# Second attention of a gated cross-attention block: VectorE's batch steps move one tick later, behind the next tile's bound, maxima and sums

## What is computed

```python
def _L1_xattn_ref(Q, K, V, mask, Wq_w, Wq_b, Wk_w, Wk_b, Wv_w, Wv_b, Wo_w, Wo_b):
    q = (Q @ Wq_w + Wq_b).reshape(b, tq, H, DK).transpose(0, 2, 1, 3)
    k = (K @ Wk_w + Wk_b).reshape(b, tk, H, DK).transpose(0, 2, 1, 3)
    v = (V @ Wv_w + Wv_b).reshape(b, tk, H, DK).transpose(0, 2, 1, 3)
    scores = jnp.einsum('bhqd,bhkd->bhqk', q, k) / jnp.sqrt(jnp.float32(DK))
    scores = jnp.where(mask == 0, jnp.float32(-1000000000.0), scores)
    attn = jax.nn.softmax(scores, axis=-1)
    out = jnp.einsum('bhqk,bhkd->bhqd', attn, v)
    return out.transpose(0, 2, 1, 3).reshape(b, tq, c) @ Wo_w + Wo_b
...
x = x + jnp.tanh(g_ffn[0]) * _L0_ffn_ref(_layernorm(x), ...)
x = x + jnp.tanh(g_xattn[1]) * _L1_xattn_ref(_layernorm(x), ctx, ctx, mask, ...)
x = x + jnp.tanh(g_ffn[1]) * _L1_ffn_ref(_layernorm(x), ...)
```

## Time and profile before

| | |
|---|---|
| median of 3 runs | 790.95 us (789.13 to 792.21) |
| the profiled execution's own time | 795.5 us |
| its span | 793.9 us |
| mean granted TensorE clock in it | 0.918 |
| PE busy | 643.7 us (81%) |
| DVE busy | 454.7 us (57%) |
| ACT busy | 307.5 us (39%) |
| POOL busy | 228.4 us (29%) |

### The profile page before, as it was taken

The page is one execution under the profiler, slowest core; times in us unless marked ns, Lnnn a source line. Parts: engine busy times, 40 slices in busy tenths (PEclk is TensorE's granted clock), DMA queues, the critical chain, the costliest instruction groups (busy, mean ns, idle before and its releaser), DMA issues. The chain is left out here.

```text
span 793.9 us, 14350 instructions
## 1 busy us (share of the span) xinstructions
PE 643.7 (81%) x4685; PEld 585.7 (74%) x4686; DVE 454.7 (57%) x1167; ACT 307.5 (39%) x533; POOL 228.4 (29%) x351
## 2 busy tenths in 40 slices
PE   3798943999999996788554757778997799999997
PEld 3566632989998996777443535558996689999997
DVE  5845555774447543000378888666657575565566
ACT  7544312552336333323453442444333323343331
POOL 7531443010001001000374854645003601011053
PEclk9999965999999999989777888788998999999999
DMA  7999316751006811655130010000006301011124
GB/s 267 417 417 410 112 41 218 249 181 51 19 20 218 311 59 40 230 195 189 49 123 9 2 53 1 1 0 1 2 1 258 107 15 53 28 53 41 38 71 155
DMA packets 23943, 93.38 MB, mean 118 GB/s; under 512 B 5073, under 2 KB 9426, under 8 KB 17922
## 3 DMA queue, kind: packets, MB, share of 16 engines
q1 hardware_dynamic: 16946, 72.28, 24.5%
q0 software_dynamic: 6960, 20.64, 8.4%
HBM read 54.37 MB, written 44.83 MB: 125 GB/s over the span
## 5 line engine op out<-in xcount | busy, mean ns | idle before, releaser
L2116 ACT ACTIVATE vz<-psum,fb 128x256 f32<-128x256 f32 x112 | 52.4, 475 | 107.5 <-PE psum L52 107.1
L1665 ACT ACTIVATE e_h<-psum,e_be 128x256 f32<-128x256 f32 x96 | 44.8, 474 | 98.2 <-PE psum L52 76.5
L1748 DVE CAST e_h_hi<-e_h 128x256 fp32r<-128x256 f32 x96 | 28.4, 295 | 67.1 <-ACT e_h L1665 66.9
L50 PE MATMUL psum<-e_h_hi,e_w_hi 128*128 128x256 f32 x192 | 54.6, 284 | 0.0
L52 PE MATMUL psum<-e_h_hi,e_w_lo 128*128 128x256 f32 x192 | 53.9, 281 | 0.0
L51 PE MATMUL psum<-e_h_lo,e_w_hi 128*128 128x256 f32 x192 | 53.9, 281 | 0.0
L2165 DVE TENSOR_TENSOR f_h_lo<-vz,f_h_hi 128x256 fp32r<-128x256 f32 x112 | 47.7, 426 | 4.0 <-DVE f_h_hi L2163 0.2
L822 POOL TENSOR_TENSOR s_sc<-s_sc,s_top 128x1024 f32<-128x1024 f32 x16 | 31.4, 1963 | 45.3 <-DVE s_top L992 45.3
L2163 DVE CAST f_h_hi<-vz 128x256 fp32r<-128x256 f32 x112 | 33.9, 303 | 15.9 <-ACT vz L2116 11.3
L1750 DVE TENSOR_TENSOR e_h_lo<-e_h,e_h_hi 128x256 fp32r<-128x256 f32 x96 | 40.9, 426 | 3.3
L50 PE MATMUL psum<-kz_hi,s_qT_hi 128*128 128x256 f32 (+1 forms) x80 | 30.6, 382 | 13.4 <-DVE s_sc L986 10.7
(11 more groups left out here) (468 smaller groups left out, 2307.2 us busy)
## 6 DMA issues: line engine op xcount, KB each, us to landing
xs<-zeros SPq DMA_DIRECT2D x18, 1024.0 KB
e_w_raw<-in_W SPq DMA_DIRECT2D x17, 1024.0 KB, 5.1
ys<-zeros SPq DMA_DIRECT2D x6, 1024.0 KB
ys<-x_norm POOLq DMA_DIRECT2D x19, 256.0 KB, 2.5
x_norm<-in_W SPq DMA_DIRECT2D x4, 1024.0 KB, 5.3
e_w_raw<-in_W SPq DMA_DIRECT2D x7, 512.0 KB, 5.1
f_w_lo<-fw SPq DMA_DIRECT2D x6, 512.0 KB
x_norm<-xs POOLq DMA_DIRECT2D x10, 256.0 KB, 3.1
```

Of the source, the lines that this page charges most:

```text
L50: nc.tensor.matmul(out, wh, xh, start=start, stop=False)
L1665: nc.scalar.activation(h32[:, m % RING], ps[:, HIDDEN_BANKS[m % RING], 0:SLOT], ACT.Gelu, bias=be[:, m:m + 1]).then_inc(gelu_ok, 1)
L1748: nc.vector.tensor_copy(h_hi[:, m], h32[:, m % RING]).then_inc(hh_ok, 1)
L2116: nc.scalar.activation(h32[:, m % RING], ps[:, HIDDEN_BANKS[m % RING], 0:SLOT], ACT.Relu, bias=b1[:, f * MH + m:f * MH + m + 1]).then_inc( ...
```

## The change

In VectorE's program, the batch steps that stood in tick n for n up to 15 now stand in tick n+1, behind `bounded(n+1)` and `reciprocals(n)`; they are put into a function `between(n)`. `q_lo` stays in its tick. From tick 16 on `between(n)` stands in its own tick; tick 16 has that of 15 and of 16. `add_rows` doesn't take the statistics any more, `sums(b, 0)` is called by itself: for batch 2 the three steps (add, statistics, chain) stand ahead of the loop, the add before `q_lo(0)` and the others behind `transposed_lo(1)`; for batch 3 they are one piece in `between(4)`, so in tick 5, ahead of `q_lo(2)`. Nothing else is changed; no instruction is added or dropped, and the other engines' programs are as they were.

```diff
@@ sums
+                if kind == 0:
+                    dve.wait_ge(xa_ok, b + 1)
...
@@ add_rows
-                dve.wait_ge(xa_ok, b + 1)
-                sums(b, 0)
...
             add_rows(0)
+            sums(0, 0)
             norm_chain(0, 0)
             add_rows(1)
+            sums(1, 0)
...
+            add_rows(2)
             dve.wait_ge(fb_ld, 32)
             q_lo(0)
             transposed_lo(1, th1_ok, tl1_ok)
+            sums(2, 0)
+            norm_chain(2, 0)
             dve.wait_ge(cap_ok, 2)
-            for n in range(TICKS):
+            def between(n):
                 b, r = divmod(n, TB)
-                if n < NT:
-                    bounded(n)
-                if 1 <= n < NT + 1:
-                    reciprocals(n - 1)
-                if r == 0 and b + 2 < B:
+                if r == 0 and 1 <= b < B - 2:
                     add_rows(b + 2)
-                if r == 1 and b + 2 < B:
+                    sums(b + 2, 0)
                     norm_chain(b + 2, 0)
-                if r == 1:
-                    if b + 1 < B:
-                        q_lo(b + 1)
-                    if 0 <= b - 2 < B:
-                        residual(b - 2)
-                        sums(b - 2, 1)
-                        norm_chain(b - 2, 1)
+                if r == 1 and 0 <= b - 2 < B:
+                    residual(b - 2)
+                    sums(b - 2, 1)
+                    norm_chain(b - 2, 1)
                 if r == 2 and 0 <= b - 3 < B:
                     logits(b - 3)
                 if r == 3:
...
+            for n in range(TICKS):
+                b, r = divmod(n, TB)
+                if n < NT:
+                    bounded(n)
+                if 1 <= n < NT + 1:
+                    reciprocals(n - 1)
+
+                if 1 <= n <= NT:
+                    between(n - 1)
+                if r == 1 and b + 1 < B:
+                    q_lo(b + 1)
+                if n >= NT:
+                    between(n)
                 if n in ROWS_AT:
```

## The result

The changed kernel takes 797.67 us in the median of 5 runs (794.75 to 799.34), the kernel before 790.95 beside it. The ratio is 1.0087, 95% interval 1.0056 to 1.0119: 6.9 us slower. The profiled execution has 797.67 us with a span of 796.1 at a mean TensorE clock of 0.900 (before: 0.918).

What follows compares the result with a forecast made beforehand. The prediction took no engine as full: a chain round the engines bounds the 16 tiles, then the drain and last layer. Its terms, -5.0 + 5.2 + 2.0 = +2.2 us on 790.95, gave 793.2 us, range 787.5 to 799.

Steps and rivals of the forecast that it cites:

- the likeliest case: Early gains spent at logits(0) with some clock loss: -2 to +4 us (789 to 794.9), chance 0.56.
- the slower rival: TensorE's clock falls at both new idle times and the early gain is not reached: +5.5 us, 796.5; chance 0.32.
- two signs of being wrong: TensorE's new wait ahead of logits(0) absent or far shorter than 5.2 us, or tile 11 not some 4 us earlier.
- Start: Tiles 0 to 2: tile 0 late by 3.4 us, net -1.7 at q_lo(1) and tile 2.
- Chain and GpSimd: VectorE's steps behind reciprocals may meet GpSimd: batch 3's add taken as 1.28 us, 0.85 kept for the range.
- Ticks 4 and 5: Tile 4 gains 1.1, sums 4 wait for the exponential, batch 3's piece is longer: +0.25 in sum, tile 6 at -1.5.
- Ticks 9 to 12: Tile 10 gains 3.9 us, tile 11 2.7, sums 10 0.8 more; project(1) and scores 14 at -5.0.
- Ticks 13 and 14: TensorE waits 5.2 us for residual(1) ahead of logits(0); scores 15 start 9.6 us behind scores 14: loss 5.2.
- TensorE's clock: Lower clock on logits(0) behind the new idle time: +2.0 us; up to 1.5 at the start left for the range.
- The faster rival: TensorE's wait in tick 13 is cheaper than its length: 787 us, 786 if all absorbed; chance 0.12.

Runs made afterwards that it cites:

- kernel 7: The changed kernel with unused products in TensorE's idle time ahead of the transposes of tiles 0 and 2 and of weighted(0); ratio 1.0026 to the kernel before.
- kernel 10: The kernel before with batch 2's norm ahead of the loop, batch 3's in one piece in tick 4, residual(0), statistics and chain behind bounds 10; ratio 0.9899.
- Kernels 1: The changed kernel with residual(1), its statistics and chain back in tick 13, ahead of bounds 14; ratio 0.9985 to the kernel before.
- 2: The changed kernel with only the add of residual(1) back in tick 13, its statistics and chain still behind bounds 14; ratio 0.9971 to the kernel before.
- 3: The changed kernel with logits(0) moved on TensorE behind the transposes of tile 12 in tick 14; ratio 0.9963 to the kernel before.
- 8: The kernel before with only residual(1), its statistics and chain moved from tick 13 behind bounds 14 and sums 13; ratio 1.0104.
- kernel 5: The kernel before with only the norms changed: batch 2's ahead of the loop, batch 3's in one piece in tick 4; 788.75 us, ratio 0.9888.
- 12: The same program as kernel 5, timed again in a later set of runs: 788.18 us, ratio 0.9963 to the kernel before.

## Why the prediction was right, and which terms were not

The forecast was 793.2 us with a range to 799.0, and the likeliest case was no measurable change; 797.67 is within the range, but on the side of the slower rival: the loss is 6.9 us for the 2.2 of the sum, and the range holds it because its upper end was that rival's. One of its two signs of being wrong also came: tile 11 is 0.3 us earlier, not some 4. Its steps in order:

- *Start.* Right: +3.4 us at tile 0. The net at tile 2 is -0.4 and not -1.7, since scores 1 came at the lower clock; the sum had put this at nothing and kept it for the range.
- *Chain and GpSimd.* Right: the chains of batches 2 and 3 take 2.0 us each, and the add of batch 3 (459.20) 1.19. The 0.85 us held for the range weren't needed on VectorE: in tick 5 the add had begun first, and GpSimd's multiplication took 2.79 us instead of 1.90. In the kernel before GpSimd had begun first, and the add took 2.13.
- *Ticks 4 and 5.* **This is the step that failed**, where it put "tile 6 at -1.5". It came at +2.0. Of the error of 3.5 us 0.5 were there at tile 4 (+56.1 against +58.4, so -2.3 for -2.8), 3.0 arose behind it. The wait of sums 4 for the exponential was foreseen, and its 3 us too. Wrong was "10.4 us behind bounds 4": it is 13.5. The working let `q_proj(2)` start when `transposed_lo(2)` is done (449.29); but it stands in TensorE's program behind the transposes of tile 2 and scores 5, which held it until 451.83. With the 2.25 us of kernel 7 it would have started at 449.75. So 0.5 us is the queue, 2.1 the clock, and about 0.7 the clock again on `q_proj(2)` itself (3.5 us for 2.8 in kernel 7). Behind it stands the second fault, of judgment: that the piece, once behind sums 4, costs its full length while the waits ahead of it stay empty was in the sum, but not that leaving it ahead of them is free (kernel 10).
- *Ticks 9 to 12.* As computed from there: TensorE waits 0.32 us ahead of scores 11 where it waited 4.31, and tile 10 is at -1.5, so it gained 3.5 for the 3.9 expected. Tile 11 is at -0.3 where the working has -4.2; from tile 9 on it gained 2.3 for 2.7, so the step holds and its start was wrong. "-5.0" at scores 14 was -2.0 (518.40 - 388.20 = +130.2, before +132.2), the error of tick 5 carried on, with half a microsecond regained.
- *Ticks 13 and 14.* Right: a wait of 5.09 us for 5.2. Kernels 1, 2, 3 and 8 show its price by four edits that have only this in common.
- *TensorE's clock.* The direction was right, the size small: +2.0 for the logits, measured +2.55 (5.21 against 2.66). The range had kept up to 1.5 us for the start, while the early ticks held some 5 by kernel 7.

With the measured terms the sum is -2.0 + 12.2 - 4.4 = +5.8 at scores 15 (in the trace +6.0), and it is +6.5 at bounds 15; the stretch has 7.5, the time 6.9. So the slower rival's number (+5.5) came near by its heading, the clock and the missed early gain. Of its three terms only the clock at the start came (the 1.3 us missing at tile 2); neither meeting with GpSimd cost VectorE anything, the piece behind tile 10 took 5.06 us (496.11 to 501.17). The rest was the clock in tick 4, which it didn't have, so its number is in part luck. The faster rival, a wait absorbed behind tick 13, is refuted: in kernel 8 scores 15 are late by the whole 12.2 - 4.4 = 7.8 us and bounds 15 by 8.9.

**What stays open.** Kernels 1 and 10 differ in the tick of the transposed and low parts and of batch 3's piece; their ratios are 0.9985 and 0.9899 in different sets of runs, while their stretches differ by 0.5 us. Bounds 6 (+77.4 against +74.4) speak for a price of the later tick of 3 us, but how much of it reaches the end wasn't isolated, and by the medians of kernel 5 the first set may flatter kernel 1. Nor is it known why the kernel before took 4.9 us more in one set than in another, or what sets the last layer's length, which varies by 10 us.

## What to carry to other kernels

A batch step has to be taken apart by who waits for it: here one add of 1.3 us releases TensorE, and the statistics and chain behind it release nobody for many microseconds. Move the second behind an engine's own next tile, and the first only where, as at `residual(0)`, nobody waits for it soon; before moving a step, look in the other engines' programs for every wait on each semaphore that it counts up, and for what is queued there behind that wait. And a step that stands in a gap in which its engine would wait anyway is free: an order that closes the gap ahead and puts the step behind it makes it cost its full length, and the idle time of TensorE that this opens is paid once more in its clock.

## What the runs showed of the hardware

- 24 products of 2 columns take 2.66 us at 2.4 GHz and 5.21 at 1.2 GHz (0.11 and 0.21 us from start to start): these small products scale with the clock almost in full.
- Unused products in TensorE's idle time made the profiled stretch 5.0 us shorter (kernel 7), and the ratio was 1.0026 for 1.0087, in different sets. The Trainium skill, page "TensorE: Matmul & The Clock Gate", section "HAM oscillation — how this bites in real kernels", names idle gaps as what throttles; the trace agrees here, with 0.99 in the idle window 520.00 to 525.10 and 0.50 in the busy one behind it, so the price shows behind the gap and not in it. A gap isn't the only way to it: in the kernel before TensorE was busy without a break from 517.50 on, was granted 1.00 in the 24 small products (520.83 to 523.49), and 0.67 in the 5.2 us behind them.
- The same program on two executions had its low-clock stretches at different ticks, and its tiles moved by up to 3 us (kernels 5 and 12). Within one attention of 213 us that is as much as most of the edits were worth.
- VectorE's add of the expert's rows (128x1024, both operands in SBUF) took 1.28 us, 2.13, 2.58 (kernel 10) and 1.19 (changed kernel, tick 5). Where GpSimd's subtraction was under way when the add began (rows 5, kernel 10), the add ended 1.1 us behind its end; in tick 5 the add began 0.16 us ahead of GpSimd's multiplication, which then took 2.79 us instead of 1.90. So one engine held the other without a semaphore, and it was the later one that paid.
